# Three more groups of edge tiles summed by dense products in the second layer of a graph block, on one core

## The chip, the cores and the metric

One core of one Trainium2 chip runs the whole kernel in one launch. The metric is the device time of that launch in microseconds (us), smaller is better. Engines are named as the profile names them: PE is TensorE (PEld its weight loads), DVE is VectorE, ACT is ScalarE, POOL is GpSimd, SP is SyncE. PE, DVE, ACT, POOL and SP each have an instruction queue of their own and meet only at semaphores.

## The reference, cut to what matters

```python
xn = _layernorm(x)                                  # 6250 nodes, 256 features
def _gcn_layer(x, W, b, src, dst, norm, n_nodes):   # 206250 edges, sorted by dst
    xt = x @ W
    msg = xt[src] * norm[:, None]
    agg = segment_sum(msg, dst, num_segments=n_nodes)
    return relu(agg + b)
norm = edge_weight * rsqrt(deg_out[src] * deg_in[dst] + EPS)
h6 = _gcn_layer(xn, W6, b6, ...)
h7 = _gcn_layer(h6, W7, b7, ...)
x = x + (h7 @ Wp + bp) + attention(xn)              # linear attention: k^T v is one 256x256 matrix
x = x + ffn(_layernorm(x))                          # top 2 of 8 experts, the same two for all rows
```

The kernel sums first and multiplies by the weight matrix afterwards, so each layer is: for every node, the weighted sum of the rows of its neighbours.

## The kernel before, in words

**Tiles.** The sorted edges make 1620 tiles of 128 edges. Two methods sum them.

*Gathered.* 1080 tiles form 45 groups (`NG`) of 24 (`GT`), a group being 6 steps (`GR`) of 4 tiles (`QT`). In a step POOL issues 4 indirect DMAs (L1854, one for each tile: 128 rows of the table into one slot of the ring `ringb`), DVE builds the selection matrices `Sb` (L1162, L1177), and PE multiplies the rows by them (`mm`, L617). The ring holds 6 steps (`RQ`): the gathers of step j wait until `mm` of step j-6 is done. After the sixth step ACT lifts the sum out of PSUM (L1635), PE transposes it (`turn`, L603), DVE adds it to `acc` (L1193).

*Dense.* The other 540 tiles form 18 chunks (`ND`) of 30. No row is gathered for them. For each tile DVE makes two one-hot matrices (`hots`: `Mb`, L1224, and `Lb` with the edge weights, L1227), PE multiplies them (`build`, L629), and ACT adds the block to the chunk's matrix A of 50 blocks of 125x128 (`evict`: six of seven columns go straight into A, L1657; the first, which may meet a column of the tile before, goes into the small ring `side`, L1661, and DVE adds it, `first_column`, L1248). A chunk is summed by 50 matmuls of A's blocks with the table held in SBUF (`dense`, L649). ACT lifts the result (L1642), PE transposes it (`dense_turn`, L659), DVE adds it (`add_chunk`, L1207).

**Two layers.** In the first layer (270 steps, 0 to 269) every chunk's A is built, multiplied, and stored to DRAM (L1911, 10 pieces of 312.5 KB). The second layer doesn't build: SP loads each A back (`load_A`, L1916) into the one buffer `A[0]`, in five parts of two DMAs. Part p of the next chunk is loaded as soon as the matmuls have used part p of this one (`refill`), and the first matmul of part p waits for that load (`l_ap`).

**Two groups are in both methods.** The groups `GX` = [20, 44] are gathered in the first layer, and their A is built there too and stored, but not multiplied (chunks 18 and 19, `DX` = 20). In the second layer these two groups are summed as chunks, so that it has 43 groups to gather, 258 steps (`NQS`), and 20 chunks. Its 1000 matmuls are spread evenly over steps 9 to 255, 4 a step. Odd and even chunks use two banks of PSUM, and the first matmul of a chunk waits until the chunk two before it was added.

**The rest of the second layer.** For each 500 finished nodes (13 such pieces) a `stream` of 17 segments, one a step, runs through all engines: scaling (L1395), hidden layer (L754), output (L766, L769), norm, transposes (L778), and DMAs in and out on SP's queue: the rows of x (L1979), stored transposes (L1980), a row of scales (L1965, half as large as the others), three results (L1987, L1990, L1993). Segment `relu0` of DVE, two steps after the loads are issued, needs the rows of x (L1399). The steps and the places of all segments follow from the group and chunk numbers; each engine runs its instructions in order of steps. After the last group come the end of the stream and the expert stage.

Of the kernel before, what the change touches and what calls it, by code (L numbers as in the profile page):

```python
# [5 lines left out]
D = 256  # L6
E = 206250
NE = 8
# [30 lines left out]
RT = 7  # L39
# [27 lines left out]
SD = 8  # L67
# [26 lines left out]
BUILD_AT = {}  # L94
for _d in range(DX):
    for _t in range(size_of(_d)):
        BUILD_AT.setdefault(_d * PD + _t * PD // size_of(_d), []).append(tile_of(_d) + _t)
FROM1 = 9
SPAN1 = NQS[1] - 2 - FROM1
# [4 lines left out]
for _d in range(DX):  # L104
    for _k in range(NT):
        MULT_AT[1].setdefault(FROM1 + (_d * NT + _k) * SPAN1 // (DX * NT), []).append((_d, _k))
FIN_AT = [{(d + 2) * PD: d for d in range(ND)}, {FROM1 + (d + 1) * SPAN1 // DX + 2: d for d in range(DX)}]
JD = [((d + 2) * PD - 3) // GR for d in range(ND)]
assert JD[-1] <= NG and max(len(b) for b in BUILD_AT.values()) <= MLS
# [19 lines left out]
CH = [list(range(ND)), sorted(range(DX), key=lambda d: FIRST_TILE["c", d])]  # L129
PARTS = [("r", j) for j in range(NR)] + [("c", d) for d in range(DX)]  # L130
# [51 lines left out]
LATE_AT = FIRST + max(KV_STEPS + 2, DX * PD - 4)  # L182
# [48 lines left out]
SPANS = [[(0, NG)], [(a + 1, b - a - 1) for a, b in zip([-1] + GX, GX + [NG]) if b - a > 1]]  # L231
# [12 lines left out]
def gnn_block(nc, srcT, srcR, dstT, dstR, dstO, wO, wT, x, W6, b6, W7, b7, Wp, bp, wkvT, woT, wq, bo, lng, lnb,  # L244
              Wr, br, W1, b1, W2, b2, gamma, beta, need, out):
    ctx = ExitStack()
    with ctx:
# [18 lines left out]
        ad = dram("ad", [DX, R, AP_])  # L266
# [28 lines left out]
        pidx = sb("pidx", [P, 1])  # L295
        ident = sb("ident", [P, P])
        ones = sb("ones", [P, P])
        eps5 = sb("eps5", [P, 1])
        eps12 = sb("eps12", [P, 1])
        eps30 = sb("eps30", [P, 1])  # L300
        nhalf = sb("nhalf", [P, 1])
# [3 lines left out]
        w6 = sb("w6", [P, 2, D])  # L305
        wkv = sb("wkv", [P, 2, 2 * D])
# [21 lines left out]
        flg = sb("flg", [1, 1], i32)  # L328
        rt = sb("rt", [1, 16, NE])
# [70 lines left out]
        psb = [PS[k][0:R, 0:HR].rearrange("p (h r) -> p h r", r=RT) for k in (2, 7)]  # L400
# [12 lines left out]
        N_WTS = 8  # L413
# [51 lines left out]
        def builds_before(s):  # L465
            return sum(len(b) for at, b in BUILD_AT.items() if at < s)

        def batches_before(s):
            return sum(1 for at in BUILD_AT if at < s)
# [17 lines left out]
        def slot_of(t):  # L487

            s = next(at for at, b in BUILD_AT.items() if t in b)
            return s % 2 * MLS + BUILD_AT[s].index(t)  # L490
# [5 lines left out]
        def chunk_bank(L, d):  # L496

            return PS[3 + L * (d % 2)]

        def tables_at(s):  # L500

            first = [chunk_of(t) for t in BUILD_AT.get(s + 1, ())]
            return [(d, k // TK) for d, k in first if k % TK == 0]
# [25 lines left out]
        def pe_program(e):  # L529
# [91 lines left out]
            def build(t):  # L621
                s = next(at for at, b in BUILD_AT.items() if t in b)
                e.wait_ge(s_M, batches_before(s) + 1)
# [5 lines left out]
                e.matmul(PS[(2, 7)[t % 2]][0:R, 0:HR], Lb[:, slot_of(t), :], Mb[:, slot_of(t), :],  # L629
                         start=True, stop=True).then_inc(s_bld, 1)  # L630

            def dense(L, d, k):
                wd = XC if L == 0 else D
                if k == 0:
# [14 lines left out]
                ins = e.matmul(chunk_bank(L, d)[:, 0:wd], lhs, X[0:R, k, 0:wd], start=k == 0, stop=k == NT - 1)  # L649
# [3 lines left out]
            def dense_turn(L, d):  # L653
                bank = chunk_bank(L, d)
# [7 lines left out]
            def sums(L, s):  # L662
                b = BUILD_AT.get(s, []) if L == 0 else []
# [47 lines left out]
            with e.If(flag != 0):  # L711
                slow_sums(0)
                e.wait_ge(s_pass, 1)
                e.sem_inc(s_bld, TDX)
# [13 lines left out]
            e.wait_ge(l_w2, 16 * 6)  # L728
# [52 lines left out]
            with e.If(flag != 0):  # L781
                slow_sums(1)
                e.wait_ge(s_pass, 2)
                for s in range(STEPS1):
                    for d, k in MULT_AT[1].get(s, ()):
                        if k % 10 == 0:
                            e.wait_ge(l_ap[k // 10], 32 * (d + 1))
                        if k % 10 == 9:
                            e.sem_inc(s_mul, 1)
# [57 lines left out]
        def dve_program(e):  # L847
# [215 lines left out]
            e.tensor_reduce(rt[0:1, 14, 0:1], sv[:, :], AX.X, ALU.max).then_inc(s_st, 1)  # L1063
            e.wait_ge(s_st, 25)
            e.tensor_copy(flg[0:1, 0:1], rt[0:1, 14, 0:1]).then_inc(s_flag, 1)
# [82 lines left out]
            def load_next(L, s):  # L1148
# [5 lines left out]
                if L == 0:  # L1154
                    for group in tables_at(s):
                        tile_columns.load(group)
# [45 lines left out]
            def add_chunk(L, d):  # L1202
# [4 lines left out]
                e.tensor_tensor(o, o, chunk_bank(L, d)[:, 0:2 * P].rearrange("p (h c) -> p h c", h=2),  # L1207
# [8 lines left out]
            def hots(s):  # L1216

                b = BUILD_AT.get(s)
# [18 lines left out]
            def first_column(t):  # L1237
# [4 lines left out]
                n = r0_before(t)  # L1242
# [4 lines left out]
                o = A[d % 2][:, :, bass.ds(tile_columns.of(t), 1)]  # L1247
# [77 lines left out]
            with e.If(flag != 0):  # L1325
                slow_sums(0)
                e.sem_inc(s_r0, TDX - DX)
# [5 lines left out]
            with e.Else():  # L1333
# [6 lines left out]
                for s in range(STEPS0):  # L1340
# [7 lines left out]
                    if s % PD == 0 and 1 <= s // PD < DX:  # L1348
                        clear(s // PD)
                    for t in BUILD_AT.get(s - 1, ()):  # L1350
                        first_column(t)
# [11 lines left out]
            e.wait_ge(l_as[1], 16 * PA * loads_of(DX, 1))  # L1363
# [6 lines left out]
            e.wait_ge(l_w2, 16 * 6)  # L1370
# [66 lines left out]
            with e.Else():  # L1437
# [4 lines left out]
                for s in range(STEPS1):  # L1442
# [688 lines left out]
```

## Time and profile before

| | |
|---|---|
| median of 3 runs | 3638.46 us (3633.55 to 3642.16) |
| the profiled execution, its own time | 3635.3 us |
| its span in the trace | 3633.3 us |
| first layer's gathers | from 447.4 us |
| second layer's gathers | from 1919.1 us to the last, issued at 3225.4 us |
| mean granted clock of PE | 0.887 of full speed |

The profile is of one execution, whose own time is 3.2 us below the median; 2.0 us of it lie outside the span. Times in views are microseconds from the start of the span.

### The profile page before, as it was taken

Reading aid. Unit: us, or ns where it says so; the run is one execution under the profiler, and the core shown is the slowest. Engines: PE = TensorE matmul, PEld = TensorE weight load, DVE = VectorE, ACT = ScalarE, POOL = GpSimd, SP = SyncE. Lnnn points to the kernel's source line nnn. Section 1 sums busy time; section 2 is a strip of 40 time slices with the busy share of each in tenths; the row PEclk is TensorE's granted clock in tenths of the full one; section 3 lists DMA queues with packets and bytes.
Section 4 is the critical chain, followed back from the end, with each engine's and each line's share of the span. In section 5 each row is a group of like instructions: output and inputs, shape, how many; then the busy total and the mean of one; then the engine's idle time right before and its main releaser. Section 6 shows DMA issues by size and latency. Waiting matters only on the chain.

```text
span 3633.3 us, 50004 instructions
## 1 busy us (share of the span) xinstructions
PE 2799.8 (77%) x15474; PEld 1797.2 (49%) x15474; DVE 1883.0 (52%) x5115; ACT 901.4 (25%) x3066; POOL 2419.4 (67%) x2355
## 2 busy tenths in 40 slices
PE   4665468989998999998754777776776777769998
PEld 4554335555555555555422444444444444435666
DVE  9999857777777777777551122221212222222334
ACT  6787542323332332332210000000000000012111
POOL 5776577777777777777766777777777777730000
PEclk8788879999999999999875788888889888979999
DMA  4110145545545555554565566666656566643221
GB/s 126 60 41 1 11 119 163 162 147 170 164 147 159 170 156 153 164 164 149 179 187 155 170 184 184 179 180 185 187 173 180 178 192 186 182 129 97 78 72 48
DMA packets 264164, 520.34 MB, mean 143 GB/s; under 512 B 65976, under 2 KB 139592, under 8 KB 263578
## 3 DMA queue, kind: packets, MB, share of 16 engines
q0 software_dynamic: 101376, 278.07, 27.4%
q1 hardware_dynamic: 156017, 232.56, 19.3%
q10 hardware_dynamic: 6500, 6.40, 0.5%
q8 instruction: 133, 2.18, 0.2%
q14 instruction: 138, 1.13, 0.1%
HBM read 407.73 MB, written 109.14 MB: 142 GB/s over the span
## 4 chain that ended last, share of the span: by engine, by line
PE 34%; POOL 30%; DVE 15%; issue 11%; DMA 7%; SPq 1%; ACT 1%; DVEq 1%; ACTq 0%; POOLq 0%
POOL ringb L1854 29%; PE ps L649 9%; PE ps L629 7%; DVE ab L1031 6%; DMA ringb<-t,src 5%; PE ps L818 5%; PE ps L831 5%; PE ps L617 3%; DVE ab L1029 3%; PE ps L578 2%; PE ps L594 1%; DVE mlb L1224 1%; POOL ab L1827 1%; SPq L1911 1%; DVE ab L1235 1%
## 5 line engine op out<-in xcount | busy, mean ns | idle before, releaser
L1854 POOL DMA_INDIRECT ringb<-t,src x2112 | 2106.4, 997 | 694.0 <-issue 624.8
L649 PE MATMUL ps<-xb,ab 125*128 125x256 f32 (+1 forms) x3800 | 1106.8, 427 | 62.1 <-ACT ab L1655 55.2
L649 PEld LDWEIGHTS ps<-xb,ab 125*128 125x128 f32 x3800 | 780.1, 213 | 372.2 <-issue 183.4
L617 PE MATMUL ps<-ringb,Sb 128*32 128x257 f32 (+1 forms) x4224 | 375.4, 431 | 434.3 <-DMA ringb<-t,src 389.8
L629 PE MATMUL ps<-mlb 128*125 128x350 f32 x1176 | 494.3, 507 | 80.1 <-DVE mlb L1224 44.4
L1657 ACT ACTIVATE ab<-ps 125x300 f32 x568 | 252.3, 444 | 667.2 <-PE ps L629 656.5
L617 PEld LDWEIGHTS ps<-ringb,Sb 128*32 128x32 f32 x4224 | 87.3, 113 | 665.9 <-DMA ringb<-t,src 531.2
L539 PE MATMUL ps<-ab 128*50 128x125 f32 x3240 | 246.6, 306 | 181.5 <-ACT ab L1585 125.6
L1827 POOL TENSOR_TENSOR ab<-ab,wn 128x100 f32<-128x100 f32 x202 | 277.2, 1378 | 125.2 <-DVE ab L1029 125.2
L1585 ACT ACTIVATE ab<-ab,wn 128x50 f32<-128x50 f32 x1216 | 297.1, 323 | 89.8 <-DVE ab L1029 88.0
L629 PEld LDWEIGHTS ps<-mlb 128*125 128x125 f32 x1176 | 209.0, 199 | 223.0 <-DVE mlb L1224 110.1
L539 PEld LDWEIGHTS ps<-ab 128*50 128x50 f32 x3240 | 206.8, 143 | 221.1 <-DVE ab L1031 188.3
L1162 DVE TENSOR_TENSOR Sb<-iof,rel 128x128 f32<-128x128 f32 x528 | 148.9, 282 | 297.2 <-PE ps L617 274.6
L1193 DVE TENSOR_TENSOR accb<-accb,ps 128x64 f32 x352 | 77.9, 221 | 408.1 <-PE ps L603 380.0
L1859 POOL TENSOR_TENSOR rs<-mv,nhalf 125x4 f32<-125x4 f32 (+1 forms) x13 | 12.8, 988 | 385.9 <-DVE mv L1550 385.9
L1224 DVE TENSOR_TENSOR mlb<-iof,rel 128x700 f32<-128x700 f32 (+2 forms) x260 | 253.2, 974 | 0.4
L1031 DVE TENSOR_TENSOR ab<-iof,ringb 128x1000 f32<-128x1000 f32 x203 | 251.1, 1237 | 0.0
L1248 DVE TENSOR_TENSOR ab<-ab,side 125x50 f32 x568 | 140.1, 247 | 159.2 <-ACT side L1661 79.9
L1227 DVE TENSOR_SCALAR mlb<-iof,src,wn 128x125 f32<-128x125 f32 x588 | 179.6, 352 | 0.0
L818 PE MATMUL ps<-xb 128*128 128x500 f32 (+1 forms) x416 | 172.0, 572 | 4.0 <-DMA Sb<-in_b 3.5
L831 PE MATMUL ps<-xb,ab 128*125 128x256 f32 x800 | 174.6, 379 | 0.0
L1177 DVE TENSOR_TENSOR Sb<-Sb,wn 128x128 f32<-128x128 f32 x528 | 156.1, 296 | 18.2
(226 smaller groups left out, 2348.4 us busy)
## 6 DMA issues: line engine op xcount, KB each, us to landing
ad<-ab SPq DMA_DIRECT2D x200, 312.5 KB
ab<-ad SPq DMA_DIRECT2D x200, 312.5 KB
ringb<-t,src POOLq DMA_INDIRECT x2112
x2t<-mlb SPq DMA_DIRECT2D x13, 500.0 KB, 4.9
xb<-x2t SPq DMA_DIRECT2D x13, 500.0 KB, 8.2
xb<-in_x SPq DMA_DIRECT2D x10, 625.0 KB
t<-xb SPq DMA_DIRECT2D x10, 625.0 KB
kvb<-t SPq DMA_DIRECT2D x50, 125.0 KB
```

Source lines behind the costliest of these rows:

```text
L539: ins = e.matmul(PS[j % 2][o:o + NT, 0:R], hot_w[:, r, j, :], hot_lo[:, r, j, :], start=t0 + j < 2, stop=t0 + j >= T - 2)
L617: ins = e.matmul(PS[g % 2][k * W:(k + 1) * W, 0:wd], Sb[:, qi % NS, k, :], msg[:, slot * QT + k, 0:wd], start=r == 0, stop=r == GR - 1)
L629: e.matmul(PS[(2, 7)[t % 2]][0:R, 0:HR], Lb[:, slot_of(t), :], Mb[:, slot_of(t), :], start=True, stop=True).then_inc(s_bld, 1)
L649: ins = e.matmul(chunk_bank(L, d)[:, 0:wd], lhs, X[0:R, k, 0:wd], start=k == 0, stop=k == NT - 1)
L818: ins = e.matmul(PS[j][:, 0:wd], M1[:, k, h, j * P:(j + 1) * P], XF[c % RF][:, h, 0:wd], start=h == 0, stop=h == 1)
L831: ins = e.matmul(pb[0:R, t * D:(t + 1) * D], hT[:, rr, m, (t0 + t) * R:(t0 + t + 1) * R], M2[:, m // 4, m % 4, :], start=m == 0, stop=m == 7)
L1031: e.tensor_tensor(hot_lo[:, r, 0:n, :], iof[:, 0:R].unsqueeze(1).to_broadcast([P, n, R]), lo_f[:, t0:t0 + n].unsqueeze(2).to_broadcast([P, ...
L1224: e.tensor_tensor(Mb[:, o:o + n, :], iof[:, 0:HR].unsqueeze(1).to_broadcast([P, n, HR]), rel[:, c0:c0 + n].unsqueeze(2).to_broadcast([P, n ...
L1585: e.activation(hot_w[:, r, j, :], hot_hi[:, r, j, :], ACT.Copy, scale=wn[:, t0 + j:t0 + j + 1]).then_inc(s_wa, 1)
L1657: e.activation(A1[d % 2][:, :, bass.ds(b, RT - 1)], psb[t % 2][:, :, 1:RT], ACT.Copy).then_inc(s_ev, 1)
L1827: e.tensor_tensor(hot_w[:, c % RD, NA:n, :], hot_hi[:, c % RD, NA:n, :], wn[:, t0 + NA:t0 + n].unsqueeze(2).to_broadcast([P, n - NA, NT]), ...
L1854: e.indirect_dma_start(msg[:, slot * QT + k, 0:width], None, table, bass.IndirectOffsetOnAxis(src[:, t:t + 1], 0)).then_inc(s_g[slot], 16)
```

## The change

Three more groups, 7, 26 and 35, become chunks of the second layer. `GX` is now [17, 44, 7, 26, 35], so there are 23 chunks (`DX`). The first 20 (`DY`), with groups 17 and 44 as the last two, are built in the first layer and stored, as before. The new three are built in the second layer, straight into `A[0]`, in the 8 steps (`YB`) after the matmuls of the chunk before them, 3 tiles a step, and multiplied from there. They are neither stored nor loaded.

- The second layer has 40 groups and 240 steps, no longer 258. The first chunk's 50 matmuls take 7 steps (9 to 15); every other chunk has 50 matmuls in 8 steps (7, 6, 6, 6, 7, 6, 6, 6) and then a step without any, 9 steps in all; the three build stages are steps 25 to 32, 132 to 139 and 185 to 192. The stream's places move with the groups: the last two pieces' begin at steps 238 and 242, not 256 and 260, and the layer's step list has 257 entries, not 275.
- The chunks in order: 0, 1, then the built one, 2 to 12 in this order (10 loads in a row after the first; one of these is group 17), the second built one, 4 loaded, the third built one, 5 loaded (the first of each run of loads is loaded while the built one is multiplied).
- All chunks use one PSUM bank (`PS[3]`); a chunk's first matmul waits until the chunk before it was added. Blocks of the second layer are built in the banks 4 and 5.
- `side` has 6 places, not 8. The edge columns have 1740 tiles, not 1668. The one-hot matrices of the second layer lie where `w6` and `wkv` were, the small constants share a tile, and the load of `br` is one of the late loads (7 DMAs, not 6).

The core of the diff:

```diff
-NX = 2
-GX = [NG * (x + 1) // NX - 1 - (x + 1 < NX) for x in range(NX)]
+NX = 5
+NY = 3
+YB = 8
+GX = [17, 44, 7, 26, 35]
 DX = ND + NX
+DY = DX - NY
-SD = 8
+SD = 6
-for _d in range(DX):
-    for _k in range(NT):
-        MULT_AT[1].setdefault(FROM1 + (_d * NT + _k) * SPAN1 // (DX * NT), []).append((_d, _k))
+FROM1 = 8
+SPAN1 = NQS[1] - 2 - FROM1 - NY * YB
+for _c, _d in enumerate(CH[1]):
+    _a = FROM1 + _n * YB + _c * SPAN1 // DX
+    if _d >= DY:
+        for _t in range(size_of(_d)):
+            BUILD_AT[1].setdefault(_a + _t * YB // size_of(_d), []).append(tile_of(_d) + _t)
+        _n, _a = _n + 1, _a + YB
+    _b = FROM1 + _n * YB + (_c + 1) * SPAN1 // DX
+    for _k in range(NT):
+        MULT_AT[1].setdefault(_a + 1 + _k * (_b - _a - 1) // NT, []).append((_c, _k))
+    FIN_AT[1][_b] = _c
...
-                    if L == 1 and d >= 2:
-                        e.wait_ge(s_add, NU[0] + ADD_NO[1]["c", CH[1][d - 2]] + 1)
-                if L == 1 and k % 10 == 0:
-                    e.wait_ge(l_ap[k // 10], 32 * (d + 1))
+                    if L == 1 and d >= 1:
+                        e.wait_ge(s_add, NU[0] + ADD_NO[1]["c", CH[1][d - 1]] + 1)
+                    if L == 1 and CH[1][d] >= DY:
+                        e.wait_ge(s_ev, tile_of(CH[1][d] + 1))
+                        e.wait_ge(s_r0, r0_before(tile_of(CH[1][d] + 1)))
+                if L == 1 and k % 10 == 0 and CH[1][d] < DY:
+                    e.wait_ge(l_ap[k // 10], 32 * loaded(d))
...
+            def hots1(s):
+                for t in BUILD_AT[1].get(s, ()):
+                    e.wait_ge(s_bld, t - MLS + 1)
+                    o, c0 = slot_of(t), TS + t
+                    e.tensor_tensor(Mb1[:, o, :], iof[:, 0:HR], rel[:, c0:c0 + 1].to_broadcast([P, HR]),
+                                    ALU.is_equal).then_inc(s_M, 1)
+                    e.tensor_scalar(Lb1[:, o, :], iof[:, 0:R], srcf[:, c0:c0 + 1], wn[:, c0:c0 + 1],
+                                    ALU.is_equal, ALU.mult).then_inc(s_L, 1)
+
+            def clear1(s):
+                for t in BUILD_AT[1].get(s + 1, ()):
+                    d, k = chunk_of(t)
+                    if k == 0:
+                        e.wait_ge(s_mul, 5 * (ND + CH[1].index(d)))
+                        e.memset(A[0][:, :, ZX:P], 0.0).then_inc(s_az, 1)
...
                     if s in FIN_AT[1]:
                         add_chunk(1, FIN_AT[1][s])
+                    for t in BUILD_AT[1].get(s - 1, ()):
+                        first_column(t)
+                    clear1(s)
+                    hots1(s + 1)
                     if s in ADD_AT[1]:
                         add(1, ADD_AT[1][s])
...
-                for p in range(5):
+                for p in range(5 if CH[1][d + 1] < DY else 0):
```

## Rows read from the trace of the kernel before

**Rows 1.** Waits (us in total, times, longest): whole span, then 1940 to 3225 us.

```profile
POOL ringb L1854 <- issue: 624.8, 2051, 0.3
...
PEld ps L617 <- DMA ringb<-t,src: 456.8, 188, 8.5
...
POOL ringb L1854 <- PE ps L617: 11.0, 36, 0.3
```

**Rows 2.** Windows: busy us (PE, PEld, DVE, ACT, POOL), PEclk, DMA share, GB/s.

```profile
1000.00:1500.00 500.00, 457.60 (x2267) 283.25 (x2260) 380.25 (x1181) 153.99 (x535) 386.98 (x372) 0.95 0.52 158
1919.00:3226.00 1307.00, 921.96 (x4715) 583.47 (x4714) 271.38 (x912) 55.20 (x143) 992.88 (x1032) 0.85 0.60 179
```

**Rows 3.** POOL's groups of instructions in the windows 1000:1500 and 2100:2600.

```profile
L1854 POOL DMA_INDIRECT ringb<-t,src x372 | 388.0, 1043 | 113.3 <-issue 111.2 <-PE ps L617 2.1
L1854 POOL DMA_INDIRECT ringb<-t,src x395 | 380.4, 963 | 120.3 <-issue 116.4 <-PE ps L617 4.0
```

**Rows 4.** Timeline: POOL's first gathers of the second layer, PE's steps 0 and 8.

```profile
1919.07 0.94 POOL L1854 DMA_INDIRECT ringb<-t,src  x1 [22.13 <-DMA t<-mbuf]
...
1929.53 1.08 PE L617 MATMUL ps<-ringb,Sb 128*32 128x256 f32 x8 [5.92 <-DMA ringb<-t,src]
...
1969.15 1.08 PE L617 MATMUL ps<-ringb,Sb 128*32 128x256 f32 x8 [4.08 <-DMA ringb<-t,src]
```

**Rows 5.** PE's timeline in the second layer: four dense products at either clock.

```profile
2104.69 0.64 PE L617 MATMUL ps<-ringb,Sb 128*32 128x256 f32 x8 [3.81 <-DMA ringb<-t,src]
...
2105.54 3.52 PE L649 MATMUL ps<-xb,ab 125*128 125x256 f32 x8
...
2201.22 2.00 PE L649 MATMUL ps<-xb,ab 125*128 125x256 f32 x8
```

**Rows 6.** Groups of instructions that make and take a block, whole span.

```profile
L629 PE MATMUL ps<-mlb 128*125 128x350 f32 x1176 | 494.3, 507 | 80.1 <-DVE mlb L1224 44.4
...
L1657 ACT ACTIVATE ab<-ps 125x300 f32 x568 | 252.3, 444 | 667.2 <-PE ps L629 656.5
...
L1248 DVE TENSOR_TENSOR ab<-ab,side 125x50 f32 x568 | 140.1, 247 | 159.2 <-ACT side L1661 79.9
L1227 DVE TENSOR_SCALAR mlb<-iof,src,wn 128x125 f32<-128x125 f32 x588 | 179.6, 352 | 0.0
```

**Rows 7.** Single lines of the kernel, min/median/max in ns: one-hot matrices, clearing of A.

```profile
L1224 DVE TENSOR_TENSOR mlb<-iof,rel x260: 510/879/1311, 446.0 to 1857.3; 128x700 f32<-128x700 f32 x92, 128x1050 f32<-128x1050 f32 x36, 128x350 f32<-128x350 f32 x2
L1235 DVE MEMSET ab<- x20: 1392/1392/2725, 444.7 to 1810.2; 125x1600 f32 x18, 125x3200 f32 x2
```

**Rows 8.** Timeline, first layer: DVE's one-hot matrices and the gathers beside them.

```profile
999.07 1.24 DVE L1224 TENSOR_TENSOR mlb<-iof,rel 128x1050 f32<-128x1050 f32 x1
1000.23 0.95 DVE L1227 TENSOR_SCALAR mlb<-iof,src,wn 128x125 f32<-128x125 f32 x3
...
999.32 1.81 POOL L1854 DMA_INDIRECT ringb<-t,src  x1 [0.30 <-issue]
```

**Rows 9.** DMA issues: count, KB each, median us to landing.

```profile
ab<-ad SPq DMA_DIRECT2D x200, 312.5 KB
...
kvb<-xtd SPq DMA_DIRECT2D x6, 500.0 KB, 18.8
```

**Rows 10.** SP's DMA queue: packets, MB, share; windows 1940:1985 and 2018:2048.

```profile
q1 hardware_dynamic: 2215, 3.18, 21.8%
...
q1 hardware_dynamic: 1097, 2.65, 23.8%
```

**Rows 11.** DVE's timeline in the prologue: an operation over all tile columns.

```profile
5.35 1.03 DVE L851 TENSOR_SCALAR rel<-src 128x1668 int32<-128x1668 int32 x1 [3.26 <-DMA src<-in_srcT]
```

**Rows 12.** Waits, second layer: DVE for the rows of x.

```profile
DVE ab L1399 <- DMA ab<-in_x: 124.0, 11, 14.8
```

**Rows 13.** Windows of 5 us: PE's clock before and after it is loaded fully.

```profile
2065.00:2070.00 5.00, 3.77 (x16) 2.05 (x15) 2.19 (x10) 0.00 (x0) 3.78 (x5) 0.50 0.58 197
2070.00:2075.00 5.00, 5.00 (x25) 3.63 (x25) 0.84 (x3) 0.38 (x1) 3.78 (x5) 0.85 0.44 124
```

More of the change, by code:

```diff
@@ L103 @@
         MULT_AT[0].setdefault((_d + 1) * PD + _k * PD // NT, []).append((_d, _k))
-for _d in range(DX):
-    for _k in range(NT):
-        MULT_AT[1].setdefault(FROM1 + (_d * NT + _k) * SPAN1 // (DX * NT), []).append((_d, _k))
-FIN_AT = [{(d + 2) * PD: d for d in range(ND)}, {FROM1 + (d + 1) * SPAN1 // DX + 2: d for d in range(DX)}]
+FROM1 = 8
+SPAN1 = NQS[1] - 2 - FROM1 - NY * YB
 JD = [((d + 2) * PD - 3) // GR for d in range(ND)]
-assert JD[-1] <= NG and max(len(b) for b in BUILD_AT.values()) <= MLS
+assert JD[-1] <= NG
 ORDER = []
@@ L129 @@
 CH = [list(range(ND)), sorted(range(DX), key=lambda d: FIRST_TILE["c", d])]
+FIN_AT = [{(d + 2) * PD: d for d in range(ND)}, {}]
+_n = 0
+for _c, _d in enumerate(CH[1]):
[8 more added lines that the diff above has]
+    FIN_AT[1][_b] = _c
 PARTS = [("r", j) for j in range(NR)] + [("c", d) for d in range(DX)]
@@ L294, in gnn_block @@
         iof = sb("iof", [P, max(HR, P)])
-        pidx = sb("pidx", [P, 1])
+        consts = sb("consts", [P, 6])
+        pidx, eps5, eps12, eps30, nhalf = (consts[:, k:k + 1] for k in range(5))
+        flg = consts[0:1, 5:6].bitcast(i32)
         ident = sb("ident", [P, P])
         ones = sb("ones", [P, P])
[L298 to L301, printed above, removed]
         scl = sb("scl", [P, NT, 2])
@@ L465, in builds_before @@
         def builds_before(s):
-            return sum(len(b) for at, b in BUILD_AT.items() if at < s)
+            return sum(len(b) for at, b in BUILD_AT[0].items() if at < s)
         def batches_before(s):
-            return sum(1 for at in BUILD_AT if at < s)
+            return sum(1 for at in BUILD_AT[0] if at < s)
         def base_col(rows):
@@ L487, in slot_of, with hots_of, bank_of, loaded @@
         def slot_of(t):
-            s = next(at for at, b in BUILD_AT.items() if t in b)
-            return s % 2 * MLS + BUILD_AT[s].index(t)
+            if t >= tile_of(DY):
+                return t % MLS
+            s = next(at for at, b in BUILD_AT[0].items() if t in b)
+            return s % 2 * MLS + BUILD_AT[0][s].index(t)
+        def hots_of(t):
+            return (Lb1, Mb1) if t >= tile_of(DY) else (Lb, Mb)
+        def bank_of(t):
+            return t % 2 + 2 * (t >= tile_of(DY))
         def r0_before(t):
             return t - sum(1 for d in range(DX) if tile_of(d) < t)
[L496 to L502, printed above, removed]
+        def loaded(c):
+            return sum(1 for d in CH[1][:c + 1] if d < DY)
+        def tables_at(L, s):
+            first = [chunk_of(t) for t in BUILD_AT[L].get(s + 1, ())]
             return [(d, k // TK) for d, k in first if k % TK == 0]
@@ L628, in build @@
                         e.wait_ge(s_c0, r0_before(t - 1))
-                e.matmul(PS[(2, 7)[t % 2]][0:R, 0:HR], Lb[:, slot_of(t), :], Mb[:, slot_of(t), :],
+                low, high = hots_of(t)
+                e.matmul(PS[(2, 7, 4, 5)[bank_of(t)]][0:R, 0:HR], low[:, slot_of(t), :], high[:, slot_of(t), :],
                          start=True, stop=True).then_inc(s_bld, 1)
@@ L1153, in load_next @@
                     load_columns("chunk", tbc, CH[L][FIN_AT[L][s + 1]], CR + SP_ - P, 1)
-                if L == 0:
-                    for group in tables_at(s):
-                        tile_columns.load(group)
+                for group in tables_at(L, s):
+                    tile_columns.load(group)
             def equal(L, j):
@@ L1347, in dve_program @@
                         add_chunk(0, FIN_AT[0][s])
-                    if s % PD == 0 and 1 <= s // PD < DX:
+                    if s % PD == 0 and 1 <= s // PD < DY:
                         clear(s // PD)
-                    for t in BUILD_AT.get(s - 1, ()):
+                    for t in BUILD_AT[0].get(s - 1, ()):
                         first_column(t)
@@ L1660, in evict @@
                     e.wait_ge(s_r0, n - SD + 1)
-                e.activation(side[0:R, n % SD, :].unsqueeze(2), psb[t % 2][:, :, 0:1], ACT.Copy).then_inc(s_c0, 1)
+                e.activation(side[0:R, n % SD, :].unsqueeze(2), bank[:, :, 0:1], ACT.Copy).then_inc(s_c0, 1)
             def scale_rows(s):
@@ L1765, in act_program @@
                         lift(1, ADD_AT[1][s + 1])
+                    for t in BUILD_AT[1].get(s, ()):
+                        evict(t)
                     for c, seg in STREAM_AT.get(s, ()):
@@ L1769, in act_program @@
                         lift_chunk(1, FIN_AT[1][s + 1])
+                    for group in tables_at(1, s):
+                        tile_columns.load(group)
             for n, o in enumerate((2, 4)):
```

90 lines of the change are left out of this document (48 added, 42 removed).

## Prediction, made before the changed kernel was timed

> **What bounds the kernel now.** I read the windows first. Over the second layer's gathers (1919 to 3226 us) POOL is busy 993 of 1307 us and PE 922 [rows 2]; neither looks full. The waits decide it: before a gather POOL sits idle for "issue", 0.305 us a time (624.8 / 2051), and for PE 36 times at 0.3 us, which is the same gap under another name [rows 1]. A gather and its gap follow each other without a break, so POOL issues as fast as it can. PE has 188 of 258 steps in which it waited for gathered rows, 457 us together [rows 1]. The 1031 intervals from 1919.07 to the last gather at 3225.4 us are 1.267 us each, 5.07 us a step [rows 4]. So the second layer's length is its number of steps times POOL's pace, and the first thing to price is the steps taken away.
>
> POOL's pace isn't constant. A gather takes 0.94 us at its shortest, 0.963 us in the mean of the second layer, 1.043 in the first [rows 3, 4], where DVE is busy 380 of 500 us [rows 2]. The timeline shows why: a gather begun at 999.32 took 1.81 us and ended at 1001.13, when DVE's three `Lb` operations (1000.23 to 1001.18) ended [rows 8]. DVE's work on SBUF lengthens a gather that lies beside it. One-hot matrices, absent from the second layer so far, are what the change brings there.
>
> **How much PE may lag.** POOL's gather count at 1969.15 us is (1969.15 - 1919.07) / 1.25 = 40, step 10; PE just then multiplies step 8, whose slot step 14 needs [rows 4]. So PE may fall 4 steps, 20 us, behind before POOL stops. A lag below that costs nothing.
>
> **Steps removed.** 18 steps x 4 gathers x (0.946 + 0.305) us = 90.1 us. I take the undisturbed gather, since the disturbance that the stream causes stays. With the mean interval it would be 91.2. The stream and the tail move by the same 18 steps.
>
> **Builds added, DVE and POOL.** 72 tiles. `Mb` of one tile 0.51 us, `Lb` 0.35 [rows 6, 7]: 61 us of DVE, and three clearings of 125x3200, 2.73 us each [rows 7], 8 us. In the first layer a gather is longer by 1.043 - 0.963 = 0.08 us for 2.2 tiles a step and other work; for 24 steps x 4 gathers that is 7.7 us. Here there are 3 tiles a step and the clearings, but no key and value work. Bounds: 0, and the whole 61 + 8 = 69 us if each such operation held POOL up in full. I take 10, near the first layer's row.
> The Trainium skill ("SBUF — State Buffer", "SBUF: two separate sides") says that the port pair shared by VectorE and GpSimd is an exclusive lock, that GpSimd can't write its descriptors meanwhile, and (in "Who interferes with whom") that `tensor_scalar` can take it, but `tensor_tensor` has no such mode. By it the 72 `Lb` operations could cost up to their own 25 us and the `Mb` nothing; the sum would end 15 us later. Rows 8 fit the `Lb` part.
>
> **Builds, the lag of PE.** DVE is busy 271 / 258 = 1.05 us a step now [rows 2]. A build step adds 3 x 0.86 for one-hot and 3 x 0.58 for `first_column` (0.25 [rows 6], and as much again and a little while one waits for the other's result): 5.4 us, against 5.1 of POOL's. PE has 0.64 to 1.08 for `mm` and 3 builds at 494 / 588 = 0.84 (two instructions each): 3.6 us; ACT has 3 x 0.44 and three small copies [rows 6]. Ahead of a stage, `clear1` waits for the last product of the chunk before; 2.73 + 0.86 us later PE gets its first tile. Queued behind that wait on DVE are `Sb` two steps on and the adds; behind PE's wait for the tile are the `mm` of later steps. The lag is 3.6 + 8 x 0.3 = 6 us a stage, under 20: nothing on the path, unless the lag is there already.
>
> **Products added.** 150 more, with the same steps' `mm` gone. Four products (8 instructions) took 2.00 us at full clock and 3.52 at half [rows 5]. PE is busy 922 / 258 = 3.57 us a step now, with 3.88 products; over the 9 steps of a chunk there will be 5.56, so 1.68 more at 0.50 to 0.88: 4.4 to 5.1 us, within POOL's 5.1. In total PE gains 150 x (0.50 to 0.88) + 72 x 0.84, less 18 x 0.64, 124 to 181 us: 86 to 91% of 1217. In the first layer it was busy 92%, and POOL's pace was still its own [rows 2, 3]. Nothing. One bank in place of two: the add has a step without products to happen in. Nothing.
>
> **The reload of A, the dear unknown.** A chunk's A is 10 x 312.5 KB = 3.2 MB; the stream moves 5 x 500 + 250 KB = 2.8 MB in some 18 steps [rows 9]. Before, a chunk had 12.35 steps (62.6 us): 5.1 MB, 82 GB/s on SP's queue. Now it has 9 (46 us with the stream's disturbance): 4.6 MB, 100 GB/s. What can the queue do? Where it had a backlog it moved 2.65 MB in 30 us, 88 GB/s, and at the layer's start 3.18 MB in 45 us, 71 GB/s, with the gathers beside it, while its packets filled only 24 and 22% of the 16 engines' time [rows 10]. At 88 a chunk takes 52.3 us, 6.3 too many. Slack: a part is reloaded some 2.6 steps after its chunk's start and needed at 9: 32 us, less 7 for its own transfer and 2 to start, 23; with the ring 43 us. The long run has 10 reloads: 63 - 43 = 20 us lost; the short ones, 4 reloads, 25 us, lose nothing. At 92 GB/s or more nothing is lost. The 88 is from A's own transfers; the stream's include some that I expect to be quicker, so I take 12, between 0 and 20. The rows of x, for which DVE waited 124 us in 11 waits even before [rows 12], will come later still; DVE is then 2 steps ahead in `Sb`, and the ring adds its 20 us.
>
> **Small things.** 72 more columns in the prologue: 1.03 us x 72 / 1668 is 0.04 for each full operation [rows 11]; with the reductions and longer rows of checks 2 us (0 to 4). `side` with 6 places: when ACT evicts tile n, tile n-6 is at least two steps old, and its `first_column` stands in DVE's queue before the one-hot matrices that tile n was made from. Nothing. The load of `br` joins a queue of six late loads that ends before the first layer does. Nothing.
>
> **Sum.** 3635.3 - 90.1 + 10 + 12 + 2 = 3569.2 against the profiled execution; the median of the runs is 3.2 above it: 3572 us, 1.8% faster.
>
> **Rivals.**
> - *SP's queue becomes the bound; slower.* At the 71 GB/s of the layer's start a chunk takes 65 us, 19 over: 10 x 19 - 43 and twice 4 x 19 - 43 are 213 us, 3770 to 3780. It gives back the whole gain from 80 GB/s down. For it: the queue was at 71 for 45 us with three quarters of the 16 engines' time left, so something narrower is full. Against: 88 later, and no wait of PE for A in the second layer before. Chance 0.10. The Trainium skill ("DMA: Bandwidth & Descriptors", "Why a DMA increments its semaphore by 16 and not by 1", on how many engines) says that a transfer of 125 rows is dealt to 5 of the 16 engines, one whose outer dimension is 4 to 4; A's loads and x's rows are such. That speaks against the change. Five engines are 31% of sixteen, so that the 22 to 24% of rows 10, with the gathers' part on top, would be nearly all of the five: the trace agrees.
> - *The build stages run serially*, DVE, PE, ACT, DVE for each tile at PE's half clock, 8 us a step: 3.6 + 8 x 2.9 = 27 us each, 7 over the ring, 21 together; after the long run of reloads the ring is spent already and it is some 20 more. 3593 to 3613. Against: three places for one-hot matrices let DVE go on. Chance 0.13.
> - *PE's clock stays low* in dense steps: 6.25 x 0.88 + 1.08 = 6.6 us and the stream's part, say 7.3, 8 of them and a free one 15 us over 46 a chunk, 300 us slower. Against: at full load the clock went from 0.50 to 0.85 of full within 5 us [rows 13]. Chance 0.02.
> - *All of it is hidden*: 3635.3 - 91 + 5 + 0, 3553 with the median's offset. Chance 0.12.
>
> **Chances.** The forecast (3560 to 3590) 0.60, the rivals 0.10, 0.13, 0.02, 0.12, no change 0.03. A measurement tells 0.2%, 7 us. Faster 0.85, same 0.03, slower 0.12. The range: at the low end everything hidden, 3549; at the high end the serial builds on a spent ring, 3613, and a little of the queue's case, 3620; out are most of the two slower rivals and the last part of no change, 0.15.
>
> **What would show it.** Right: the second layer's gathers end 75 to 80 us earlier; gathers of 1.3 us and more cluster in the three build stages; PE busy 86 to 91%; POOL's waits for PE are few and lie at the end of the run of 10 reloads. Wrong: PE waiting at L649 for `ab<-ad` in each chunk, SP's queue at 90 GB/s or less without pauses, POOL idle for PE for more than 40 us; or PE's builds waiting for DVE so long that steps of a build stage take 8 us.

## The result, and the profile after

The changed kernel takes 3650.78 us (median of 20 runs, 3640.89 to 3659.93), the kernel before 3639.26 us beside it (20 runs, 3629.75 to 3645.77). The ratio is 1.0031, with a 95% interval of 1.0021 to 1.0040: slower by 0.3%, where 1.8% faster was forecast. The profiled execution after took 3657.94 us, its span 3656.1.

Four moments cut both profiles into the same pieces: the first gather, the first gather of the second layer, the last gather, the end. Of after, the line of POOL's gathers (min/median/max in ns, first and last start), and the timeline where the layers meet (start, duration, engine, line):

```profile
L1907 POOL DMA_INDIRECT ringb<-t,src x2040: 942/949/4439, 523.8 to 3252.2; - x186
```

```profile
1990.08 0.95 POOL L1907 DMA_INDIRECT ringb<-t,src  x1 [0.30 <-issue]
2013.08 0.95 POOL L1907 DMA_INDIRECT ringb<-t,src  x1 [22.05 <-DMA t<-mbuf]
```

In the kernel before the same line gives 447.4 and 3225.4, and [rows 4] the 1919.07.

| us | before | after | difference |
|---|---|---|---|
| start to the first gather | 447.4 | 523.8 | +76.4 |
| to the second layer's first gather | 1471.7 | 1489.3 | +17.6 |
| to the last gather | 1306.3 | 1239.1 | -67.2 |
| to the end | 407.9 | 403.9 | -4.0 |
| span | 3633.3 | 3656.1 | +22.8 |

The second layer did what was forecast (-68). What ate it lies 1500 us earlier, ahead of the first gather, in a stage whose code the diff hardly touches.

**The first layer's start.** SP's timeline of the changed kernel, at its beginning (start, and how long SP stayed with the issue of one DMA):

```profile
7.19 5.65 SPq L1921 DMA_DIRECT2D accb<-in_dstR  x1
12.88 15.33 SPq L1922 DMA_DIRECT2D ringb<-in_dstT  x1
...
31.40 1.98 SPq L1924 DMA_DIRECT2D kvb<-in_dstO  x1
33.43 31.72 SPq L1925 DMA_DIRECT2D mbuf<-in_wO  x1
65.19 34.48 SPq L1927 DMA_DIRECT2D wb<-in_W  x1
...
122.42 1.00 SPq L1935 DMA_DIRECT2D minsd<-Sb  x1
```

SP stood at two issues for 31.7 and 34.5 us; in the kernel before the same two took 0.49 and 0.43 us, and the store of `minsd` was issued at 46.29 us. It is 76.1 us later now, and the first gather 76.4. The chain of work that ended last names the same two issues without any comparison. Among its longest pieces (start, us, what) stand

```profile
33.43 31.72 SPq L1925
65.19 34.48 SPq L1927
...
2481.99 25.14 DMA ab<-in_x
```

**The second layer.** The window of its gathers, in the columns of [rows 2]; then the groups of PE's dense products and of POOL in it, and its waits:

```profile
2013.00:3252.00 1239.00, 944.33 (x5017) 626.48 (x5016) 332.83 (x1084) 92.77 (x284) 937.44 (x959) 0.90 0.57 181
```

```profile
L676 PE MATMUL ps<-xb,ab 125*128 125x256 f32 x2300 | 596.8, 410 | 22.6 <-DMA ab<-ad 20.7 <-DVE ab L1292 1.0 <-issue 0.7
...
L1907 POOL DMA_INDIRECT ringb<-t,src x959 | 937.4, 978 | 323.4 <-issue 280.6 <-DMA t<-mbuf 22.1 <-PE ps L637 20.8
```

```profile
DVE ab L1443 <- DMA ab<-in_x: 228.5, 10, 41.4
...
POOL ringb L1907 <- PE ps L637: 20.8, 38, 4.6
```

POOL is still the bound: it stood for PE 38 times, 20.8 us, of which 38 x 0.305 = 11.6 are the gap that every gather has [rows 1] and 9.2 are stalls. A gather takes 978 ns in the mean; it was 992.88 / 1032 = 962 [rows 2]. DVE's wait for the rows of x went from 124.0 [rows 12] to 228.5 us. PE is busy 76% of the window, with more products than before, whose group in the same window of the kernel before is

```profile
L649 PE MATMUL ps<-xb,ab 125*128 125x256 f32 x2000 | 610.6, 453 | 0.0
```

Three gathers are long (3.50, 4.24 and 4.44 us), one beside each of the three clearings of `A[0]`; one of them in the timeline:

```profile
2721.36 4.24 POOL L1907 DMA_INDIRECT ringb<-t,src  x1 [0.30 <-issue]
...
2721.68 2.73 DVE L1272 MEMSET ab<- 125x3200 f32 x1 [6.21 <-PE ps L676]
```

### The profile page after: what moved, and what is told of

The parts are those of the page before. It is cut to its first block, busy times and chain, and to the rows that moved or that the text cites. A ratio compares the mean times of both kernels' runs of the same rounds, so it can differ in the third digit from the quotient of the medians.

```text
span 3656.1 us, 51405 instructions
## 1 busy us (share of the span) xinstructions
PE 2827.3 (77%) x15774; PEld 1847.2 (51%) x15774; DVE 1945.7 (53%) x5286; ACT 937.5 (26%) x3207; POOL 2376.9 (65%) x2283
## 4 chain that ended last, share of the span: by engine, by line
PE 34%; POOL 25%; DVE 15%; issue 10%; DMA 7%; SPq 5%; DVEq 2%; ACT 1%; ACTq 1%; POOLq 0%
POOL ringb L1907 24%; PE ps L676 9%; PE ps L653 7%; DVE ab L1058 5%; PE ps L845 5%; PE ps L858 5%; DMA ringb<-t,src 4%; PE ps L637 3%; DVE ab L1056 3%; DMA ab<-in_x 2%; PE ps L598 2%; SPq L1927 1%; PE ps L614 1%; DVE mlb L1250 1%; SPq L1925 1%
## 5 line engine op out<-in xcount | busy, mean ns | idle before, releaser
L1907 POOL DMA_INDIRECT ringb<-t,src x2040 | 2065.1, 1012 | 686.5 <-issue 602.1
L676 PE MATMUL ps<-xb,ab 125*128 125x256 f32 (+1 forms) x4100 | 1095.3, 405 | 88.7 <-ACT ab L1704 56.0
L676 PEld LDWEIGHTS ps<-xb,ab 125*128 125x128 f32 x4100 | 807.2, 202 | 370.8 <-issue 177.7
L637 PE MATMUL ps<-ringb,Sb 128*32 128x257 f32 (+1 forms) x4080 | 346.3, 413 | 293.9 <-DMA ringb<-t,src 195.0
L1706 ACT ACTIVATE ab<-ps 125x300 f32 x637 | 283.9, 446 | 739.8 <-PE ps L653 693.9
L1912 POOL TENSOR_TENSOR rs<-mv,consts 125x4 f32<-125x4 f32 (+1 forms) x13 | 12.9, 989 | 382.7 <-DVE mv L1598 382.7
L1292 DVE TENSOR_TENSOR ab<-ab,side 125x50 f32 x637 | 157.5, 247 | 179.9 <-ACT side L1710 89.8
L858 PEld LDWEIGHTS ps<-xb,ab 128*125 128x125 f32 x800 | 150.0, 188 | 27.1 <-issue 5.1
```

The costliest lines, as they stand in the source:

```text
L637: ins = e.matmul(PS[g % 2][k * W:(k + 1) * W, 0:wd], Sb[:, qi % NS, k, :], msg[:, slot * QT + k, 0:wd], start=r == 0, stop=r == GR - 1)
L676: ins = e.matmul(PS[3][:, 0:wd], lhs, X[0:R, k, 0:wd], start=k == 0, stop=k == NT - 1)
L858: ins = e.matmul(pb[0:R, t * D:(t + 1) * D], hT[:, rr, m, (t0 + t) * R:(t0 + t + 1) * R], M2[:, m // 4, m % 4, :], start=m == 0, stop=m == 7)
L1706: e.activation(A1[place][:, :, bass.ds(b, RT - 1)], bank[:, :, 1:RT], ACT.Copy).then_inc(s_ev, 1)
L1907: e.indirect_dma_start(msg[:, slot * QT + k, 0:width], None, table, bass.IndirectOffsetOnAxis(src[:, t:t + 1], 0)).then_inc(s_g[slot], 16)
```

## The experiments

The suspect for the 76 us is a line that the diff doesn't contain. `RG = -(-TA // GW)`, with 16 tiles to a row (`GW`), gives the number of rows of `dstR`, `dstO` and `wO`, three tensors of the stage ahead of the first gather (the prologue) with RG rows on RG partitions. TA, the number of tiles in the edge columns, went from 1668 to 1740, RG from 105 to 109. 105 is 15 x 7; 109 is prime.

Experiments 1 to 4 ran on one chip (before: 3641.66 us), 5 to 8 on a second (4046.27), 9 to 11 on a third (4075.33), 12 on a fourth (3634.91). On the second and third every kernel was slower, and POOL stood for other engines in the gathers of both layers there. A time or an interval is compared within one chip, unless the text says otherwise.

**1 and 3: before, with 109 rows and with 112.**

```
-RG = -(-TA // GW)
+RG = 109          # experiment 3: 112
```

> The kernel before with one number changed: the three tensors of destinations and weights (dstR, dstO, wO) and the two small stores of the bounds have 109 rows in place of 105 (the last four are padding). Theory: the changed kernel's first gather came 76 us later because these transfers, with 109 rows, are given to one DMA engine, and all else of the prologue's loads waits behind them on SP's queue; then this kernel is slower than before by 65 to 85 us, all of it ahead of the first gather (at about 520 us in place of 447), and its minsd store is issued near 120 us in place of 46. Rival: the delay came from the 72 more columns of one-hot and bounds work or from the moved br load; then this kernel is within 5 us of before.

> Control: the kernel before with 112 rows in place of 105. If the number of rows matters through the count of DMA engines alone, 105 rows (15 engines) and 112 rows (16) differ by at most 2 us, and the time is 3635 to 3642 us. If more rows as such cost time, it is slower by several us, as a share of what 109 rows cost.

With 109 rows 3713.44 us, ratio 1.0200 (1.0186 to 1.0214); with 112 rows 3641.76 us, ratio 1.0005 (0.9996 to 1.0014). Nothing but the number of rows differs, and no tile is added. POOL's gathers and SP's timeline with 109 rows:

```profile
L1854 POOL DMA_INDIRECT ringb<-t,src x2112: 945/949/2023, 523.1 to 3302.4; - x192
```

```profile
33.56 31.54 SPq L1872 DMA_DIRECT2D mbuf<-in_wO  x1
...
122.91 0.54 SPq L1883 DMA_DIRECT2D minsd<-Sb  x1
```

The first gather comes at 523.1 us, as in the changed kernel (523.8); with 112 rows it comes at 447.5. That is the whole 76 us. Why SP stands is in the row of DMA throughput, the first 200 us in 40 slices of 5 us, with 109 rows:

```profile
GB/s 206 208 115 77 28 52 162 26 26 26 27 30 26 26 30 26 28 26 26 26 74 121 28 93 78 19 158 106 108 66 60 99 101 0 12 98 109 43 0 14
```

and with 112 rows:

```profile
GB/s 224 198 162 248 261 240 207 77 0 74 130 97 112 37 2 71 100 89 0 22 99 110 32 0 23 99 109 33 48 94 112 7 93 99 69 11 98 112 37 25
```

With 112 the loads run at 162 to 261 GB/s and are over after 40 us. With 109 the core moves 26 to 30 GB/s from 35 to 100 us, about a tenth of that. The three tensors are 2.6 MB (873 KB each), and 2.6 MB at 26 GB/s are 100 us. All later loads are queued behind them.

The windows show how many DMA engines work. Their last three numbers are PE's clock, the mean busy share of the core's 16 DMA engines, and GB/s. First 109 rows from 35 to 100 us, then 112 rows from 15 to 35 us:

```profile
35.00:100.00 65.00, 17.88 (x208) 16.57 (x208) 27.07 (x44) 21.54 (x81) 17.97 (x13) 0.58 0.07 27
```

```profile
15.00:35.00 20.00, 13.52 (x178) 12.01 (x180) 20.00 (x32) 16.44 (x69) 13.02 (x11) 0.99 1.00 239
```

A share of 0.07 of 16 engines is 1.1 engines; a share of 1.00 is all 16.

By the Trainium skill ("DMA: Bandwidth & Descriptors", "Why a DMA increments its semaphore by 16 and not by 1") a transfer runs on k engines, the largest k up to 16 that divides its rows: 15 for 105, 1 for 109, 16 for 112. The runs agree, in time and in the busy share; and the flat 26 GB/s lies just under the 27.2 that the skill ("SBUF — State Buffer", "The DMA setup-cost knee") gives for one of the 16 ports.

**2: the changed kernel with 112 rows.** The same one-line edit.

> The changed kernel with one number changed: the same three tensors and two stores have 112 rows in place of 109. Theory of the one engine: the first gather comes at 445 to 455 us, and the time is 3565 to 3585 us, faster than before by 55 to 75 us (1.5 to 2.0%). Rival (72 columns or the moved load are the cause): 3640 to 3660 us, as the changed kernel.

3575.79 us (5 runs), ratio to before 0.9809 (0.9792 to 0.9825). The first gather comes at 448.7 us, the second layer's at 1934.02, the last at 3171.1: the second layer's gathers take 1237.1 us. All that the change was forecast to give is there; the time is 4 us from the forecast. The other possible causes (72 more columns, the moved load of `br`) are bounded by the first gather: 448.7 against 447.5 with 112 rows in the kernel before, 1.2 us for both.

**5: before, with 111 rows** (3 x 37).

> The kernel before with 111 rows in place of 105 in the same three tensors and two stores. 111 is 3 times 37. Theory (the rows are shared among as many engines as the largest number up to 16 that divides them, the Trainium skill, page Why a DMA increments its semaphore by 16 and not by 1): 3 engines. With 109 rows on 1 engine the first gather came 75.6 us late; if the delay goes with rows per engine, it is between nothing (the engines' work still ends before it is wanted) and a third of that, 25 us, and a row of the three tensors lands in about a third of the time that it took with 109. Rival (only a prime count, or any odd count above 105, is slow): as with 109 rows, 70 to 78 us.

Ratio 1.0016 (0.9992 to 1.0040). SP's timeline and POOL's gathers:

```profile
15.13 7.04 SPq L1872 DMA_DIRECT2D mbuf<-in_wO  x1
22.22 12.11 SPq L1874 DMA_DIRECT2D w<-in_W  x1
...
56.51 0.83 SPq L1883 DMA_DIRECT2D minsd<-Sb  x1
```

```profile
L1854 POOL DMA_INDIRECT ringb<-t,src x2112: 940/946/2024, 455.6 to 3645.8; - x192
```

The store of `minsd` comes at 56.5 us, 10 later than with 105 rows (46.29, on another chip), the first gather 7.9 us later than in a kernel with 112 rows on the same chip (experiment 7, 447.7). So neither an odd count as such nor one above 105 is slow: with three engines the delay is about a tenth of that with one. While these loads run, the DMA engines are busy as three of 16 (0.19) would be, and a little more:

```profile
20.00:35.00 15.00, 8.70 (x137) 6.95 (x134) 15.00 (x26) 11.54 (x48) 9.52 (x8) 1.00 0.21 83
```

That the delay is a tenth and not a third fits the thought that most of their work still ends before it is wanted; no run separates that.

**4: experiment 2, with the reload of A cut by rows.** 112 rows and 13, in place of two halves of the columns.

```
-for q in range(2 * p, 2 * p + 2):
-    e.dma_start(ab[0:R, q * PW:(q + 1) * PW], ad[d][:, q * PW:(q + 1) * PW]).then_inc(l_ap[p], 16)
+for lo, hi in ((0, 112), (112, R)):
+    e.dma_start(ab[lo:hi, 2 * p * PW:2 * (p + 1) * PW],
+                ad[d][lo:hi, 2 * p * PW:2 * (p + 1) * PW]).then_inc(l_ap[p], 16)
```

> The second kernel of this set, and the reload of the dense matrix A in the second layer is cut by rows (0 to 111, and 112 to 124) in place of by columns, still two transfers for each tenth pair, same bytes. Theory: A's 125 rows go to 5 engines, and the reload holds SP's queue and with it the loads of x and xT (DVE waited 228 us for in_x in the changed kernel, 124 before); with most of A on 16 engines this wait falls to 100 to 150 us and the second layer shortens by 5 to 15 us. Rival: what SP's queue delays is covered, and the layer is set by POOL's gathers alone: within 3 us of the second kernel of this set, whatever the wait for in_x does.

3570.07 us, ratio 0.9810 (0.9796 to 0.9824); by the ratios not told from experiment 2 (0.9809). The profiles, one of each, do tell them apart. Waits of the second layer in experiment 2, then here:

```profile
DVE ab L1443 <- DMA ab<-in_x: 217.9, 10, 38.8
PE ps L676 <- DMA ab<-ad: 22.8, 7, 12.3
...
POOL ringb L1907 <- PE ps L637: 21.5, 54, 3.9
```

```profile
DVE ab L1443 <- DMA ab<-in_x: 49.0, 8, 9.4
...
POOL ringb L1907 <- PE ps L637: 3.4, 11, 0.3
```

PE no longer waits for A, DVE waits 49 us for x in place of 218, and POOL's stalls are gone: 3.4 / 11 is the ordinary gap. The layer's gathers take 3162.1 - 1931.49 = 1230.6 us, 6.5 less. So the reload did hold the layer, by 5.0 us of stalls in experiment 2 (21.5 less 54 x 0.305) and 9.2 in the changed kernel; most of the 218 us of waiting was covered. What made the reload quicker is not separated: cut by rows, most of A goes in transfers of 112 rows, and each row's piece is also twice as long (5 KB, no longer 2.5), so that SP's queue had 45522 packets in place of 56171 for the same 97 MB (1935 to 3160 us).

**6 and 7: the stores of A cut by rows too, in the changed kernel and in before.** In the first layer the memset of a chunk's A waits once for a store of A, and POOL stands once for PE, until about 10 us after that memset has begun: 13.0 us in experiment 2, 12.8 in experiment 4, 7.3 in experiment 3 (the kernel before). The memset in experiment 2:

```profile
L1279 DVE MEMSET ab<- x20: 1392/1392/2725, 445.9 to 1824.1; 125x1600 f32 x18, 125x3200 f32 x2
its engine sat idle before it (us, times) until:
  DMA ad<-ab: 20.3, 1
```

The edit, the same in both kernels:

```
-o = d % 2 * AP_ + p * PW
-e.dma_start(ad[d][:, p * PW:(p + 1) * PW], ab[0:R, o:o + PW]).then_inc(l_as[d % 2], 16)
+q, (lo, hi) = p // 2 * 2 * PW, ((0, 112), (112, R))[p % 2]
+o = d % 2 * AP_ + q
+e.dma_start(ad[d][lo:hi, q:q + 2 * PW], ab[lo:hi, o:o + 2 * PW]).then_inc(l_as[d % 2], 16)
```

> The changed kernel with 112 rows in the prologue, A's reload cut by rows, and now the stores of A in the first layer cut by rows as well (0 to 111 and 112 to 124, two column parts at a time, same count of transfers). Near 1832 us POOL stood 12.8 us for PE, PE for DVE's one-hots, and DVE for the store of A to DRAM (17.3 us before, 20.3 us with the change) ahead of its clearing of A. Theory: that chain makes the stall, and with the stores on 16 engines it goes: 8 to 13 us less than the kernel with the reload alone cut, 3555 to 3563 us. Rival: the wait is for the order of SP's queue, and the stall stays: within 3 us.

> Control: the kernel before with 112 rows and with both the stores and the reload of A cut by rows. Its stall for the same store is 7.3 to 8.0 us long. Theory: 7 to 8 us less in the first layer and 0 to 7 us less in the second (reload), so 3625 to 3636 us; the distance to the changed kernel with the same edits stays 65 to 75 us. Rival (the cuts help only where groups are built in the second layer): as before, 3638 to 3644 us.

3965.76 us, ratio 0.9801 (0.9775 to 0.9826), and 4043.91 us, ratio 0.9998 (0.9981 to 1.0015). In both the wait for the store is no longer among the memset's; in experiment 5, uncut on the same chip, it was 6.8 us. The kernel before gained nothing (7 to 15 us were expected), and the two are 78 us apart (65 to 75 expected). The price can't be read here: on this chip POOL stood for PE and others all through the first layer. It is read from experiment 12.

**8, 10 and 12: experiment 6, with the three clearings of the second layer on ACT.**

```
-e.memset(A[0][:, :, ZX:P], 0.0).then_inc(s_az, 1)                                      # DVE
+e.activation(A[0][:, :, ZX:P], A[0][:, :, ZX:P], ACT.Copy, scale=0.0).then_inc(s_az, 1) # ACT
```

> The sixth kernel (112 rows, stores and reload of A cut by rows), and the three clearings of A in the second layer move from DVE's memset (2.73 us each) to ACT, as a copy with scale 0 of the same part. In the changed kernel the gather beside each of these memsets took 3.4 to 4.4 us in place of 0.95, 8 to 9 us in all. Theory (DVE's memset holds POOL's work on the descriptors up): these three gathers take 1.0 to 1.6 us, the layer is 6 to 9 us shorter. Rival (the gathers are long because of what else goes on there, PE's change to a new group or the DMA engines' load): the three stay long and the time the same within 3 us.

> The eighth kernel again: 112 rows in the prologue, A's stores and reload cut by rows, the three clearings of the second layer on ACT. On the chip of its first timing all kernels ran about 11% longer than on the one before, with POOL's gathers standing for PE in the first layer as well, so its size is not yet known for a chip where the gathers set the pace. From the parts: 3570 (reload cut) less 12.8 (stall for the store of A) less 8 (three long gathers) gives 3549 us, 2.5% faster than before; rival (the stall's 12.8 us come back as waits elsewhere): 3560 to 3566 us.

> The eighth kernel a third time, to have its size where POOL's gathers alone set the pace of the first layer (kernel before near 3640 us), which the last two chips did not show. There: 3549 us (3544 to 3555), from 3570 less 12.8 for the stall and less 8 for the three long gathers; rival, that the stall's time comes back elsewhere: 3560 to 3566 us. Where the kernel before takes over 4000 us, the ratio is 0.976 to 0.981 as before and tells nothing new.

Beside experiment 6 on its chip the first of them is 8 us less, 3957.59 us, with intervals that overlap. In the profiles the second layer's gathers take 1387.2 us with the clearings on ACT and 1394.3 in experiment 6 (7.1 less); on the third chip they take 1399.3 in experiment 10 and 1405.1 in experiment 11 (5.8 less). The ratios are 0.9777 (0.9751 to 0.9803), 0.9787 (0.9769 to 0.9806) and 0.9746 (0.9732 to 0.9759); the last is 3541.87 us beside 3634.91, 93 us less than before. Its gathers, and the idle time of the memset that is left on DVE and of ACT's copy:

```profile
L1907 POOL DMA_INDIRECT ringb<-t,src x2040: 942/946/2017, 448.5 to 3132.0; - x186
```

```profile
L1271 DVE MEMSET ab<- x20: 1392/1392/2725, 445.7 to 1802.0; 125x1600 f32 x18, 125x3200 f32 x2
its engine sat idle before it (us, times) until:
  issue: 13.6, 19
  DMA ad<-ab: 2.3, 1
...
L1709 ACT ACTIVATE ab<-ab x3: 2869/2870/2870, 2046.1 to 2863.5; 125x3200 f32<-125x3200 f32 x3
```

The longest gather takes 2.0 us, with the memsets it was 4.2 to 4.6 (4.50 in experiment 6, on the chip of experiment 8). From first gather to the second layer's it is 1467.3 us (1915.82 less 448.5), 15.5 less than in experiment 4, on another chip; the stall of 12.8 us that experiment 4 had is not there, and where the layers meet POOL waits 19.5 us, no longer 21.9. The second layer's gathers take 1216.2, 14.4 less than in experiment 4, of which the three gathers beside the memsets are 8; the two pairs on one chip give 6 to 7. Both theories of the parts hold. The time is 7 us below the 3549 expected, but so is the kernel before on this chip (3634.91 against 3641.66): the expected ratio was 3549 / 3641.66 = 0.9745, the measured one is 0.9746.

**9: the changed kernel again, beside 10 and 11.**

> The changed kernel itself, unedited, beside the next two kernels on one chip, so that the distance from it to them is read directly. As at its first timing: 0.2 to 0.4% slower than before.

4072.35 us, ratio 0.9999 (0.9978 to 1.0020), so not the 0.2 to 0.4% that was expected. Its profile there: first gather at 523.4 us, 74.9 later than experiment 10's 448.5. The loss of the prologue is the same each time it was seen (74.9 to 76.4 us). That the ratio is nearer to 1 fits a second layer that gives more back where its steps are longer: its gathers take 85 us less in experiment 6 than in experiment 7, on the second chip, where the changed kernel had 67 us less.

**11: experiment 6, with a small copy ahead of each memset.**

```
+e.tensor_copy(slow[:, 6:7], iof[:, 0:1])
 e.memset(A[0][:, :, ZX:P], 0.0).then_inc(s_az, 1)
```

> The sixth kernel (112 rows, stores and reload of A cut, clearings on DVE's memset) with one small DVE copy (128 by 1, from SBUF to SBUF) ahead of each of the three memsets in the second layer. In the first layer the same memset, to the same addresses, ran twice beside gathers of 0.95 us; there the DVE work ahead of it was an addition with PSUM as one operand, in the second layer a product of two SBUF operands (Sb by wn). Theory (what DVE ran last decides whether its memset holds POOL up): the three gathers take 0.95 to 1.6 us, and the time is that of the tenth kernel within 3 us. Rival (it is the memset itself in this place, whatever ran before): 3.4 to 4.5 us as before, and the time 6 to 9 us above the tenth kernel.

3993.27 us, ratio 0.9794 (0.9773 to 0.9814), not told from experiment 10 by its time. The theory falls by its gathers (4.43, 4.05 and 4.31 us), the first of them:

```profile
2330.27 0.15 DVE L1272 COPY slow<-iof 128x1 f32<-128x1 f32 x1 [6.86 <-remote]
...
2330.53 4.43 POOL L1908 DMA_INDIRECT ringb<-t,src  x1 [0.30 <-issue]
...
2331.04 2.73 DVE L1273 MEMSET ab<- 125x3200 f32 x1 [0.62 <-issue]
```

The gather beside the memset is as long with another operation just ahead of it.

## Why the prediction was wrong

- **The step that failed** is "Small things": "72 more columns in the prologue: 1.03 us x 72 / 1668 is 0.04 for each full operation [rows 11]; with the reductions and longer rows of checks 2 us (0 to 4)". It measured 76.4. The operations were priced rightly (1.2 us between experiments 2 and 3). What was left out is that the count of tiles also sets the shape of three loads, and that each of them, with a prime number of rows, went to one DMA engine (busy share 0.07 of 16, experiment 1). The range (3549 to 3620 us) had no room for it, because no rival lay ahead of the first gather at all. The rule that gives it was quoted in the prediction, for A's 125 rows; it was not asked of the transfers whose row count the change moves.
- **Steps removed**, -90.1: 72 intervals less at the mean of 1.267 us are -91.2. Right.
- **Gathers made longer by DVE**, +10: (978 - 962) ns x 960 are 15. The size is near, the share of the parts is not. The three gathers beside the clearings are 9.3 us longer than an undisturbed one. The other 79 gathers of the three build stages took at most 1.29 us and are 4.2 us over 0.946 each in all, so the one-hot matrices, 61 of the 69 us of DVE's work that was priced, cost 4 us at the most. The 15 us more that the prediction allowed for the `Lb` operations, by the rule on the shared port pair that it cites, did not come.
- **Reload of A**, +12 (0 to 20): 9.2 us of stalls of POOL for PE, in three stalls from 2616 to 2715 us (steps 118, 135 and 136), at the end of the run of 10 reloads, as forecast. Right in size and place. That the number of DMA engines sets the rate is argued: experiment 4 took the stalls away by another cut of A, which changed the length of the pieces too. That x's rows go to 4 engines, as the prediction has it, no run shows.
- **Products added**, nothing on the path: right, but the sum for PE, 86 to 91% busy, was wrong: 944 of 1239 us, 76%. The granted clock of the window was 0.90, where it had been 0.85, and a product's instruction took 410 ns in place of 453: 2300 of them took 596.8 us where 2000 had taken 610.6. The higher clock paid for the added work; the prediction had priced the additions alone and left the rest of PE's work at its old clock.
- **The layer as a whole**: -91.2 + 15 + 9.2 = -67; measured -67.2, forecast -68.
- **First layer**, forecast as unchanged: +17.6. POOL's gathers of this layer, before and after:

```profile
L1854 POOL DMA_INDIRECT ringb<-t,src x1080 | 1113.1, 1031 | 357.8 <-issue 321.7 <-DMA t<-scl 21.4 <-PE ps L617 14.7
```

```profile
L1907 POOL DMA_INDIRECT ringb<-t,src x1080 | 1125.9, 1043 | 362.7 <-issue 321.2 <-DMA t<-scl 21.4 <-PE ps L637 20.1
```

  Of the 17.6 us, 12.8 are longer gathers (1125.9 less 1113.1) and 4.8 longer idle time, nearly all of it POOL's stalls for PE (12.6 us in all, 8.0 before), which experiment 12 took away. The same two parts between experiments 3 and 2, on one chip, are 3.2 and 5.8 of 9.0. The gathers' part varies with the execution (1113 to 1118 us in three profiles of the kernel before with different numbers of rows, 1119 to 1126 in four of the changed one); whether the change lengthens them, and why the stall is longer, stays open.
- **Rivals**: none was the cause. The serial build stages didn't come (POOL's longest wait for PE was 4.6 us), nor did the queue decide, nor did PE's clock stay low (0.90), nor was all of it hidden (24 us of the gain were lost in the layer).
- **The signs**: the second layer's gathers took 67 us less, not 75 to 80; of the 21 gathers of 1.3 us and more only the three beside the clearings lay in the build stages; PE was busy 76%; POOL's stalls for PE lay where they were said to.

## What to carry to other kernels

When a change moves a size, follow that size into every tensor whose shape is worked out from it, in the stages that the diff doesn't show too, and look at the number of rows of each transfer: 105 to 109 rows cost 76 us on 2.6 MB, and padding to 112 cost nothing. A DMA throughput that stays flat at a tenth of its usual level, a busy share of one in 16, and an issuing queue that stands 30 us at one issue, are how it looked in the profile. Where a whole gain is missing and the changed stage measures as forecast, compare the start times of the stages before looking for a subtle cause.

## What the hardware showed that was not expected

- Rows and DMA engines: with 109 rows 26 to 30 GB/s and a busy share of 0.07 for 65 us; with 111 rows a share of 0.21 and 8 us of delay; with 105 and 112 rows no delay.
- A memset of 125x3200 on DVE (2.73 us) made the gather beside it 3.3 to 4.6 us long in the second layer, in 18 of 18 cases (six profiles), each ending 1.19 us after the memset, and the same work on ACT (2.87 us) did not. In the first layer a memset of the same shape, once to the same part of A, left its gathers at 0.94 to 0.97 us (but for one of 1.8 in experiment 7). The Trainium skill ("SBUF — State Buffer", "SBUF: two separate sides") says of the port pair shared by VectorE and GpSimd that who comes second is blocked for the whole of the other's instruction, and a gather that ends 1.19 us after the memset fits a blocked one, though most of these gathers began before it. It also says ("Who interferes with whom") that an operation with at most one SBUF input outside the two-port modes does not contend; the first layer agrees, the second doesn't. What tells the two layers apart is open; what DVE ran just before is not it (experiment 11).
- The same kernel took 3635 to 3642 us on two chips and 4046 and 4075 on two others. With 112 rows the prologue is as long on all four (first gather at 447 to 449 us) and the gathers are as short (946 to 949 ns in the median), but POOL is idle before its gathers for 1122 us in experiment 5 where it was 694 in the kernel before. PE's granted clock was lower there too (0.844 against 0.887 in the mean). What makes these chips slower stays open.
